# Two chained recurrent layers on one core: layer 1 six steps behind layer 0 instead of seven, its projection moved, and a new order of the first loads

## What is computed

```python
xW = einsum('ntd,dh->nth', x, Wx) + b
h  = tanh(h_prev @ Wh + xW[t])      # t = 0 .. 1023, h0 = cond_1024
x  = x + hs                         # then the same again with layer 1
```

## Time and profile before

| | |
|---|---|
| median of 3 runs | 2060.2 us (2059.27 to 2060.22) |
| the profiled execution | 2059.4 us |
| its span in the trace | 2057.6 us |
| granted TensorE clock | 1.00 of full speed |
| PE matmul busy | 2044.6 us (99%) |
| PE weight load busy | 1863.8 us (91%) |
| DVE / ACT / POOL busy | 1746.3 (85%) / 1280.9 (62%) / 444.9 us (22%) |

### The profile page before, as it was taken

One profiled execution on the slowest core, in us unless ns is written; L12 is line 12 of the kernel. 1 busy time (PEld: TensorE's weight loads), 2 busy tenths in 40 slices (PEclk: granted clock), 3 DMA queues, 4 the chain that ended last, 5 costly groups with the idle time before them and its releaser, 6 DMA issues.

```text
span 2057.6 us, 219078 instructions
## 1 busy us (share of the span) xinstructions
PE 2044.6 (99%) x98388; PEld 1863.8 (91%) x98388; DVE 1746.3 (85%) x10221; ACT 1280.9 (62%) x6660; POOL 444.9 (22%) x2054
## 2 busy tenths in 40 slices
PE   8999999999999999999999999999999999999999
PEld 6999999999999999999999999999999999999997
DVE  5888888888888888888888888888888888888887
ACT  4666666666666666666666666666666666666665
POOL 3222222222222222222222222222222222222221
DMA  3000000000000000000000000000000000000000
GB/s 108 25 26 25 26 25 26 25 26 25 27 24 27 24 28 24 28 24 28 24 27 24 27 24 27 24 27 24 28 23 28 23 27 24 27 24 27 24 27 15
DMA packets 111960, 56.33 MB, mean 27 GB/s; under 512 B 12432, under 2 KB 111008, under 8 KB 111520
## 3 DMA queue, kind: packets, MB, share of 16 engines
q1 hardware_dynamic: 111168, 53.53, 8.8%
q10 hardware_dynamic: 576, 1.18, 0.2%
q0 software_dynamic: 32, 0.02, 0.0%
HBM read 37.90 MB, written 16.78 MB: 27 GB/s over the span
## 4 chain that ended last, share of the span: by engine, by line
PE 99%; DMA 1%; issue 0%; DVE 0%; ACT 0%; SPq 0%; ACTq 0%
PE ps_rec L270 44%; PE ps_rec L287 33%; PE ps_xw L247 22%; DMA wx<-wx_in 0%; DMA wh<-wh_in 0%; PE ps_rec L339 0%; DVE zt L463 0%; ACT h L387 0%; SPq L223 0%; ACTq L421 0%; ACTq L420 0%; DVE z L472 0%; DVE x_out L503 0%; SPq L222 0%
## 5 line engine op out<-in xcount | busy, mean ns | idle before, releaser
L270 PE MATMUL ps_rec<-wh,h 128*32 128x128 f32 x33024 | 1261.2, 273 | 3.3 <-ACT h L387 2.8
L387 ACT ACTIVATE h<-z 128x24 f32<-128x24 f32 x4066 | 654.7, 208 | 666.4 <-DVE z L472 625.0
L287 PE MATMUL ps_rec<-wh_part,h 128*32 128x128 bf16 x48792 | 1036.9, 219 | 1.5 <-issue 1.5
L270 PEld LDWEIGHTS ps_rec<-wh,h 128*32 128x32 f32 x33024 | 880.0, 109 | 30.1 <-ACT h L387 6.7
L287 PEld LDWEIGHTS ps_rec<-wh_part,h 128*32 128x32 bf16 x48792 | 724.0, 96 | 151.1 <-issue 1.8
L205 POOL TENSOR_TENSOR h<-h 128x16 f32<-128x16 f32 x2032 | 430.6, 212 | 1589.9 <-DVE h L205 1589.9
L472 DVE TENSOR_REDUCE z<-zt 128x24 f32<-128x72 f32 x4066 | 664.5, 205 | 69.7 <-DVE zt L463 0.6
L376 ACT ACTIVATE ps_rec<-ps_xw,mask 128x128 f32<-128x128 f32 x2048 | 664.2, 324 | 77.9 <-PE ps_xw L247 77.9
L463 DVE STREAM_TRANSPOSE zt<-ps_rec 128x128 f32<-128x128 f32 (+1 forms) x2063 | 649.8, 316 | 18.7 <-PE ps_rec L270 12.7
L205 DVE TENSOR_TENSOR h<-h 128x16 f32<-128x16 f32 x2034 | 356.0, 175 | 209.2 <-ACT h L387 0.2
L247 PE MATMUL ps_xw<-wx,x_pe 128*32 128x128 f32 x8248 | 404.6, 273 | 2.0 <-issue 1.1
(11 more groups left out here) (20 smaller groups left out, 16.5 us busy)
## 6 DMA issues: line engine op xcount, KB each, us to landing
x_pe<-x_t SPq DMA_DIRECT2D x256, 64.0 KB, 2.0
x_dve<-x_t SPq DMA_DIRECT2D x256, 64.0 KB, 1.9
out_t<-x_out SPq DMA_DIRECT2D x256, 64.0 KB, 1.5
wh<-wh_in SPq DMA_DIRECT2D x1, 1024.0 KB, 5.7
wx<-wx_in SPq DMA_DIRECT2D x1, 1024.0 KB, 8.3
wx<-wx_in ACTq DMA_DIRECT2D x1, 512.0 KB, 5.2
wx<-wx_in SPq DMA_DIRECT2D x1, 512.0 KB, 5.0
wh<-wh_in SPq DMA_DIRECT2D x1, 512.0 KB, 7.2
```

Source lines behind the costliest of these rows:

```text
L270: mm = pe.matmul(rows(ps_rec[l][n % 2], g), h_step(l, n - 1)[:, k, :], wh[l][:, k, g * P:(g + 1) * P], start=False, stop=k == KC - 1 and n ...
L287: mm = pe.matmul(rows(ps_rec[l][n % 2], g), h_bits(l, n - 1)[:, k, :], wh_part[l][:, i, at:at + P], start=False, stop=k == KB[l] - 1 and i ...
L387: act.activation(h_of(l, n)[:, tiles, :], src[:, tiles, :], ACT.Tanh).then_inc(h_count(l, n)[0], 1)
```

## The change

Layer 1 runs six slots behind layer 0. Its four projection pieces stand in slots 4c + 4 and 4c + 5, both halves; those of layer 0 in the two slots after. PE now waits on `mid_done` before the first piece of every group, and DVE counts that semaphore down once per group. On ACT, `begin(1, 4c)` moves from the end of slot 4c + 5 to ahead of layer 1's tanh in that slot; the wait for the loaded x moves ahead of layer 0's tanh. SP's load of DVE's x waits for a transpose of layer 0 in place of `mid_done`. Wh1 is loaded in halves around Wx1 without the wait for Wh0; the first bias moves to SP, h_first to ACT, layer 1's seeds behind slot 1. POOL prepares Wh parts in another order. One of the two warm-ups between the first matmuls goes, and slot 0 does the fourth projection piece of group 1.

```diff
-LAG = RING - 1
-WARM = (10, 3, 3)
+LAG = RING - 2
+WARM = (10, 3)
-PROJECT = (((0, 3), (1, 0)), ((1, 1), (1, 2)), ((1, 3), (0, 0)), ((0, 1), (0, 2)))
+PROJECT = (((1, 0), (1, 1)), ((1, 2), (1, 3)), ((0, 0), (0, 1)), ((0, 2), (0, 3)))
...
# SP
+            sp.dma_start(bias[0][:, :], weights[0][2]).then_inc(s_bias[0], DMA)
             sp.dma_start(wh[0][:, tiles, :], weights[0][1][:, tiles, :]).then_inc(s_wh0[0], DMA)
             sp.dma_start(x_pe[1][:, :], x[:, 1, :]).then_inc(x_first[1], DMA)
-            for c in range(2):
-                load(x_dve, x_dve_loaded, c)
+            load(x_dve, x_dve_loaded, 0)
             sp.wait_ge(proj_done[0], 1)
             load(x_pe, x_pe_loaded, 2)
-            for e in s_wh0:
-                sp.wait_ge(e, DMA)
-            sp.dma_start(wh[1][:, :, :], weights[1][1]).then_inc(s_wh1, DMA)
+            sp.dma_start(wh[1][:, tiles, :], weights[1][1][:, tiles, :]).then_inc(s_wh1[0], DMA)
             sp.dma_start(wx[1][:, :, :], weights[1][0]).then_inc(s_wx1, DMA)
+            tiles = HALVES[1]
+            sp.dma_start(wh[1][:, tiles, :], weights[1][1][:, tiles, :]).then_inc(s_wh1[1], DMA)
+            load(x_dve, x_dve_loaded, 1)
...
-                    sp.wait_ge(mid_done, c - 1)
+                    sp.wait_ge(zt_done[0], zt_count(0, S4 * (c - 1)))
                     load(x_dve, x_dve_loaded, c)
...
# PE
-                for k in range(in_parts(l, n), KC):
+                tiles = (2, 3, 0, 1) if (l, n) == (0, 0) else range(in_parts(l, n), KC)
+                for k in tiles:
...
-                    if k == 0 and l == 1 and c in (0, NG - 1):
-                        pe.wait_ge(mid_done, c + 1)
+                    if k == 0 and l == 1:
+                        pe.wait_ge(mid_done[c % 2], 1)
                     project(l, c, k)
...
-                    for k in range(KC - 1):
+                    for k in range(KC):
                         project(0, 1, k)
...
-                        pe.wait_ge(s_wh1, DMA)
+                        pe.wait_ge(s_wh1[1], DMA)
...
-                if k % 2:
-                    warm(ps_rec[1][1], WARM[k // 2 + 1])
+            warm(ps_rec[1][1], WARM[1])
...
# ACT
                 for l in LAYERS:
+                    if l == 0 and s % S4 == 1 and 2 <= (c := (s + 7) // S4) < NG:
+                        act.wait_ge(x_pe_loaded[c % 2], DMA * (c // 2))
+                    if l == 1 and s % S4 == 1 and s > S4 and (n := number(1, s + 1)) is not None and n:
+                        begin(1, n)
                     if (n := number(l, s)) is not None:
                         tanh(l, n)
...
                     if (n := number(l, s + 2)) is not None and n >= 2:
-                        begin(l, n)
+                        if l == 0 or n % S4:
+                            begin(l, n)
...
# POOL
-            pool.dma_start(h_first[:, :], h_init).then_inc(s_first, DMA)
-            for l in LAYERS:
-                for k in range(KB[l]):
+            for l, k in ((0, 0), (1, 0), (1, 1), (0, 1)):
...
# DVE
                 if t == S4 - 1:
-                    add.then_inc(mid_done, 1)
+                    add.then_inc(mid_done[c % 2], 1)
...
+                if n0 is not None and s % S4 == 2 and s > S4:
+                    dve.sem_inc(mid_done[(s // S4 - 1) % 2], -1)
```

More of the change, by code:

```diff
@@ L96, in build @@
         s_wh0 = [sem(f"wh0_loaded{i}") for i in range(2)]
-        s_wh1 = sem("wh1_loaded")
+        s_wh1 = [sem(f"wh1_loaded{i}") for i in range(2)]
         s_wrest = [sem(f"wh_rest{l}_made") for l in LAYERS]
@@ L119, in build @@
         split_done = [[sem(f"split{l}_done{j}") for j in range(2)] for l in LAYERS]
-        mid_done = sem("mid_done")
+        mid_done = [sem(f"mid_done{j}") for j in range(2)]
         out_done = sem("out_done")
@@ L271, in recur_whole @@
                                        wh[l][:, k, g * P:(g + 1) * P], start=False,
-                                       stop=k == KC - 1 and not in_parts(l, n), skip_group_check=True,
+                                       stop=k == tiles[-1] and not in_parts(l, n), skip_group_check=True,
                                        tile_position=(0, 32 * g))
@@ L398, in slot @@
                         act.sem_inc(done, -count)
-                    if l == 0 and s % S4 == 1 and 2 <= (c := (s + 7) // S4) < NG:
-                        act.wait_ge(x_pe_loaded[c % 2], DMA * (c // 2))
                     if (n := number(l, s + 2)) is not None and n >= 2:
-                        begin(l, n)
+                        if l == 0 or n % S4:
+                            begin(l, n)
                     elif l == 1 and s + 2 == LAG + 1:
@@ L420, in _ @@
             act.dma_start(wx[0][:, tiles, :], weights[0][0][:, tiles, :]).then_inc(s_wx0[1], DMA)
-            act.dma_start(bias[0][:, :], weights[0][2]).then_inc(s_bias[0], DMA)
+            act.dma_start(h_first[:, :], h_init).then_inc(s_first, DMA)
             act.dma_start(wh[0][:, tiles, :], weights[0][1][:, tiles, :]).then_inc(s_wh0[1], DMA)
@@ L426, in _ @@
             act.wait_ge(s_marked, 1)
-            for l in LAYERS:
-                act.wait_ge(s_bias[l], DMA)
-                for c in range(2):
-                    seed(l, c).then_inc(s_seed, 1)
-                if l == 0:
-                    act.wait_ge(s_mask, 1)
-                    begin(0, 0)
-                    begin(0, 1)
+            act.wait_ge(s_bias[0], DMA)
+            for c in range(2):
+                seed(0, c).then_inc(s_seed, 1)
+            act.wait_ge(s_mask, 1)
+            begin(0, 0)
+            begin(0, 1)
             for s in range(T + LAG):
                 slot(s)
+                if s == 1:
+                    act.wait_ge(s_bias[1], DMA)
+                    for c in range(2):
+                        seed(1, c)
         @block.gpsimd
@@ L440, in _ @@
             pool.memset(h[1][:, :], 0.0).then_inc(s_clear, 1)
-            pool.dma_start(h_first[:, :], h_init).then_inc(s_first, DMA)
-            for l in LAYERS:
-                for k in range(KB[l]):
-                    pool.wait_ge(s_wh0[0] if l == 0 else s_wh1, DMA)
-                    at = slice(k * D, (k + 1) * D)
-                    full, left = wh[l][:, k, :], wh_rest[l][:, at]
-                    pool.tensor_tensor(left, full, upper(full), ALU.subtract).then_inc(s_wrest[l], 1)
-                    pool.tensor_copy(wh_part[l][:, 0, at], upper(full)).then_inc(s_wpart[l], 1)
-                    pool.wait_ge(s_wrest[l], k + 1)
-                    pool.tensor_copy(wh_part[l][:, 1, at], upper(left)).then_inc(s_wpart[l], 1)
-                    pool.tensor_tensor(wh_part[l][:, 2, at], left, upper(left), ALU.subtract).then_inc(s_wpart[l], 1)
+            for l, k in ((0, 0), (1, 0), (1, 1), (0, 1)):
+                pool.wait_ge(s_wh0[0] if l == 0 else s_wh1[0], DMA)
+                at = slice(k * D, (k + 1) * D)
+                full, left = wh[l][:, k, :], wh_rest[l][:, at]
+                pool.tensor_tensor(left, full, upper(full), ALU.subtract).then_inc(s_wrest[l], 1)
+                pool.tensor_copy(wh_part[l][:, 0, at], upper(full)).then_inc(s_wpart[l], 1)
+                pool.wait_ge(s_wrest[l], k + 1)
+                pool.tensor_copy(wh_part[l][:, 1, at], upper(left)).then_inc(s_wpart[l], 1)
+                pool.tensor_tensor(wh_part[l][:, 2, at], left, upper(left), ALU.subtract).then_inc(s_wpart[l], 1)
             for l, n in ORDER:
```

## The result

The changed kernel takes 2113.0 us (median of 4 runs, 2112.2 to 2113.1), the kernel before 2059.9: ratio 1.0257, 95% interval 1.0245 to 1.0270. It is slower, as forecast, but by 53 us instead of 26.5, and so above the upper end of the range.

The account below looks back on a forecast made before the run. PE was taken as full, with both layers' loops just in time. 254 x (0.07 + 0.04) = 27.9, start -0.4 + 0.35, end -1.36 gave +26.5 us; with the median 0.8 above the profiled execution, 2086.7 us, range 2068 to 2108.

Parts of the forecast that it names:

- PE has no idle time in a half-slot: PE in the middle: matmul issue fills each 0.99 us half-slot, so any stall is lost at every occurrence.
- The rival in which PE takes the waits in: PE in the middle: it has room and absorbs both waits; 2058.8 us, no change; chance 0.13.
- The wait for x ahead of tanh 0: ACT, slot 4c + 5: waits for a load issued slots before, so it costs nothing.
- First wait: PE, first half of slot 4c + 4: layer 1's first projection piece waits for mid_done; 0.07 us in each of 254 groups.
- Second wait: ACT, slot 4c + 5: begin ahead of layer 1's tanh makes it 0.06 late; 0.04 us PE stall a group.
- The doubled version: Rival: layer 0's transpose on DVE is pushed behind the late rest, second wait 0.12 a group; 2107 us; chance 0.11.
- Warm-up removed lies in that wait: Start: the first recurrence waits for Wh0 at 9.07 anyway, so removed warm-up, bias and h_first queue changes cost 0.
- The end, -1.36: End: one lone slot of layer 1 goes, 1.70 us, part given back in slots 1024 and 1025; net -1.36 us.
- PE's count of matmuls is unchanged: PE, listed under what costs nothing: the same number of matmuls, but for the one warm-up.

Follow-up runs that it names:

- a1: Changed kernel with ACT's wait for the loaded x put back behind layer 0's tanh, where it was: 2096.6 us, ratio 1.0183.
- b1: Kernel before with only the wait for the loaded x moved ahead of layer 0's tanh: 2073.2 us, ratio 1.0070.
- b5: Changed kernel with both waits at tanh 0, the one for z first in the code and that for x behind it: 2095.9 us, ratio 1.0184.
- d3: a1 with each group's last sum_mid done by POOL behind its rest instead of by DVE: 2070.3 us, ratio 1.0057.
- e1: Changed kernel with x wait back, each group's last sum_mid on POOL, first bias and h_first on their old queues: 2070.2 us, ratio 1.0053.
- f2: e2 with 18 warm-up matmuls fewer ahead of the first projection, which moves PE's loop body: 2060.0 us, ratio 1.0004 to the kernel before.
- a4: Changed kernel with x wait back, layer 1's first projection piece from the mask (mid_done awaited one piece later), and seed 0 of 32 columns: 2069.0 us, ratio 1.0050.
- e2: e1 with layer 0's seed on 32 of 128 columns: 2069.2 us, ratio 1.0050.
- e3: Changed kernel with layer 1's first piece from the mask and an always satisfied wait in place of the one for x_mid: 2100.9 us, ratio 1.0202.
- a6: Changed kernel with layer 0's bias and h_first loaded on their old queues: 2109.9 us, ratio 1.0250.
- c3: Kernel before with only the new projection table and what it needs, including the mid_done wait and its count-down on DVE: 2094.0 us, ratio 1.0173.
- c5: c3 with the count-down of mid_done issued by ACT instead of DVE: 2082.9 us, ratio 1.0118.
- f1: Kernel before with 18 more warm-up matmuls ahead of the first projection, which moves PE's loop body: 2059.1 us, ratio 1.0001.
- f3: e3 with 18 warm-up matmuls fewer ahead of the first projection, which moves PE's loop body: 2086.1 us, ratio 1.0132.
- a3: Changed kernel with layer 0's seed of 32 columns instead of 128 from the third group on: 2101.2 us, ratio 1.0207.

## Why the prediction was right in direction and wrong in size

- *"PE has no idle time in a half-slot: it is full ... Any wait that stops PE for a moment is therefore lost for good."* Right, and the main reason. Each of the three pauses of 0.05 to 0.09 us came back in full in the time, and each went when its cause was removed. The rival in which PE takes the waits in (2058.8) is refuted. The Trainium skill, "Perfetto Trace Analysis", section Identifying the Most-Contended Engine, would judge PE's room by the weight loads' busy share (and by MFU, the share of peak arithmetic, which wasn't worked out here). The trace doesn't agree: the loads are busy 90% in the changed kernel, and the other 10% took in nothing.
- *"The wait for x ahead of tanh 0 is for a load issued slots before."* **This step failed.** The sum put this wait at nothing because the load has long landed. That is true and beside the point: the cost is that the wait for z, which comes last, is pushed off the ACTIVATE, and tanh 0 starts 0.06 late. It measured 0.055 a group, 14 to 16 us in a1, b1 and b5, against 0: more than half of what was missing.
- *First wait, "I take 0.07".* Right mechanism (load 0.05 after the sum, as forecast), too small: 0.092, or 23 us instead of 18. 0.068 is the wait itself. The other 0.024 stands one step on, between this piece and the whole step behind it (0.242 instead of 0.218), where the sum had no term; the 0 to 0.025 that I had was for load to matmul, and is 0.00 in the rows above.
- *Second wait, 0.04.* Right: 0.046 by the medians, 10.3 us by the short seed, and 0.037 with tanh 1 0.06 late, as forecast, where the x wait is gone (a1, d3). The doubled version, "the transpose of layer 0 ... is pushed as well", isn't seen. Its total of 2107 came nearest of all rivals, by the wrong road.
- *"Warm-up removed lies in that wait, and so do the bias and h_first that change queues: 0."* Wrong by some 1.4 us in the profiled execution: the first full half-slot's parts start at 26.37 instead of 24.99, +1.38 instead of -0.05. The bias comes late, PE stands, and the clock falls. Where it doesn't fall, the term is about 0, as forecast; how often it falls isn't known.
- *The end, -1.36.* Right: from layer 0's last parts to the end it is 15.31 us instead of 16.66, -1.35, and there are six lone slots.
- *Not in the sum at all:* the late loads behind the loop's branch. "PE's count of matmuls is unchanged, but for the one warm-up" counts them (98392 against 98388 by the page) and not where they stand: 36 more lie ahead of the loop. In the changed kernel PE waits for the sum in that same half-slot, so most of the delay is covered; it is seen only once the first wait is gone. Of the 4 us that the medians leave, 1.4 are in half-slot 0, where the mean is 0.0055 above the median, and the rest is spread over half-slots 2 to 6. How much of this is the delay stays open: no run has the changed kernel with its body moved.

The measured terms: 23.4 + 14.0 + 11.7 + 1.4 - 1.4 = 49.1, and 4 outside the medians, against 53.1 measured. The forecast had 17.8 + 0 + 10.2 - 0.05 - 1.4 = 26.5.

**No version beats the kernel before.** The most that the change can win is its one lone slot, some 1.3 us in 2059. e1 is +11.3 us; f2 is level with the kernel before, but leaves three quarters of seed 0 out, and e1 with its body moved wasn't tried. There would be little to gain: e1's half-slots 0 lose under 1 us in all.

## What to carry to other kernels

Where one engine is full and others hand over to it just in time, count what a move costs at the hand-over: the producer's end, plus the way of the semaphore, against the grid of the consumer's starts, plus its restart, times the number of occurrences. Let the wait that is satisfied last be the one that the instruction itself carries (here the one written first; the trace shows which it is), and treat no added wait as free until the chain that it joins is shown to have slack. Compare the average period by counting events in a long window, since busy shares don't show pauses of 0.1 us; and when a removed cost doesn't come back in full, look at what happens behind the loop's branch before doubting the sum.

## What the runs showed of the hardware that I had not expected

- Of two waits ahead of one ACTIVATE, the one written first is on the ACTIVATE in the records, and the other on a semaphore instruction ahead of it. Where that other one is satisfied last, tanh starts 0.33 behind the reduction, where it is satisfied early 0.27 to 0.28.
- With PE's loop body of 768 pairs 36 pairs later, the 14th load behind the branch came at 0.49 to 0.54 us instead of 0.36 in a1 to a4, e2 and e3 (9 us in e2, 15 in e3), and at 0.41 to 0.42 in the changed kernel, a6, b5, d3 and e1, whose bodies lie at the same place; 8 or 18 pairs later (c3, c5, f1 to f3) it came at 0.36 to 0.37. Why just this load, and what rule it follows, stays open.
- A body twice as long was fetched anew in every pass, 14.6 MB, and the time rose 1.55 times.
- One more semaphore instruction per group on DVE brought a stall of 0.30 us every 64 us, 11 us in all, in c3; in the changed kernel, which has it too, the stall came twice.
- Behind 2.7 us of idle PE the granted clock was 0.50 between 8.5 and 10.5 us and 0.71 on average over 2 more; with 0.9 us of idleness it stayed at 1.00. The length of the idle time alone doesn't decide it: e3's clock fell behind 2.39 us, a3's stayed at 1.00 behind 2.62.
- A 128x32 sum took 0.26 us on POOL against 0.18 on DVE, and DVE lost nothing beside it.
